# Int8 cross-attention stage of a two-layer Perceiver kernel: norm and queries made inside the stage, its context loaded during the FFN, transfers issued inside norms and attention, FFN units and turns in another order

## The chip, the cores and the metric

The kernel runs on one core of a Trainium2 chip. The metric is the device time of one execution in microseconds (us). The engines are named as in the profile: PE (TensorE), DVE (VectorE), ACT (ScalarE), POOL (GpSimd) and SP (SyncE, which only issues transfers here).

## What is computed

Two layers work on 256 tokens of 512 features, with a context of 4096 rows of 512 features. Each layer is a cross-attention over the context, a self-attention and an FFN, each behind a layernorm and with a residual.

```
x = x + L0_xattn(ln(x), ctx)   # fp8 projections, 16 heads of 128; self part (8 groups) and context part
x = x + L0_attn(ln(x))         # causal, 16 heads of 128
x = x + L0_ffn(ln(x))          # MXFP8 blocks of 32, 512 -> 2048 -> 512
x = x + L1_xattn(ln(x), ctx)   # int8, 16 heads of 32
x = x + L1_attn(ln(x))         # lightning attention with decay
x = x + L1_ffn(ln(x))          # mixture of 32 experts
```

The int8 attention, in whose stage most of the change lies:

```
q = x @ Wq + bq ; k, v = split(cond @ Wkv + bkv) ; q = q * 32**-0.5
q, k = fq_sym(q, per row of 32), fq_sym(k, per row of 32) ; v = fq_sym(v, per column over the context)
attn = fq_unsigned(softmax(q k^T), per row, 255 levels)
out  = (attn @ v) @ Wp + bp
```

## The kernel before

The program is a chain of stages. A stage allocates its SBUF and PSUM tiles and its semaphores, runs one block with a queue of instructions for each engine, and ends with a clearing of its semaphores and a barrier of all engines (`Stage.__exit__`). A plain block ends in a barrier too. Within a block engines meet only at semaphores, and each executes its queue in the order written.

The stages that the change touches, in order of time:

- `self_attention_stage` (self part of the first cross-attention, 133 to 198 us). A stage `ctx_load` stands ahead of it, whose block only has SP issue five transfers: the first weights and the 8 MB context for the wide stage.
- `wide_cross_attention_stage` (199 to 1172 us). 8 groups of 2 heads by 8 chunks of 512 context rows give 64 steps n; a step on PE is half of the key and value projection of chunk n, the transposes of chunk n-1's keys, the other half, `weigh` of chunk n-10, and the scores of chunk n-1. In the last group (n from 56) only keys are projected and the values come ten steps later. DVE measures and normalises keys, subtracts peaks (`shift`), keeps a running maximum (`top`), adds sums from step 66, and rounds 24 units of the later FFN's weights, each in two halves (`scale_unit`, `round_unit`) in successive steps. The halves stand in steps whose number modulo 8 is 4 to 7, 0 or 1, from step 4 to step 65. Units 21 to 23 are in steps 60 to 65. ACT copies projections and scores out of PSUM and takes roots and exponentials. POOL adds exponentials. SP loads a unit, stores it when it is rounded, and reloads q and the weights for each group.
- `build_middle`: a block that only issues the causal stage's first seven transfers; `layernorm_stage` "ln1"; the causal attention; "ln2"; `ffn_stage`. The FFN has 8 steps: `gate_up(n)` on PE, an exponential on ACT, 13 DVE instructions which end in a rounded tile, `turn` (4 transposes) and its copy, and `down(n)`. Turns 0 and 1 are of the FFN's input, and `gate_up(0)` waits for both.
- `build_int8_attention`: stage `ctx2`, whose block issues ten transfers (query, key and value weights and again the 8 MB context) while DVE clears `qrows`; `layernorm_stage` "ln3"; `int8_queries_stage` (query product, rounding, three copies as parts, 32 transposes, copies to `qrows`); `int8_cross_attention_stage`, then the projection.

In `int8_cross_attention_stage` all engines walk one list, `int8_order`. It opens with the first chunk's keys and values: for n from 0 to 7 a key product of 512 rows (PE) into the one PSUM tile `vp`, its bias add ("key kept") and rounding (DVE), its parts (ACT and POOL), a value product (PE), its copy (ACT) and peak (DVE), and from n = 3 the transposes of the keys of three steps before. The next key product waits for the last "key kept". Then come scores ("first": a maximum on DVE; "second": an exponential on ACT).

Of the kernel before, what the change touches and what calls it, by code (L numbers as in the profile page):

```python
# [162 lines left out]
def self_attention_stage(nc, C, qT, kT, v, inv_smooth, cat):  # L163
# [5 lines left out]
    with Stage(nc, "self") as st:  # L169
# [15 lines left out]
        with nc.Block() as block:  # L185

# [91 lines left out]
def wide_cross_attention_stage(nc, C, ctxT, s_ctx, w, s_w, wkv_dram, q_dram, vecs, inv_smooth, cat, units, early):  # L278
# [19 lines left out]
    UPG = FFN_EARLY // NG  # L298
    with Stage(nc, "wide") as st:
# [32 lines left out]
        with nc.Block() as block:  # L332

            @block.sync
            def _(sp):
# [9 lines left out]
                for g in range(NG):  # L345
                    if g >= 1:
                        sp.wait_ge(s_s, 4 * QPG * g)
                    sp.dma_start(q[:, :], q_dram[:, 2 * g:2 * g + 2, :].rearrange("p h n -> p (h n)")).then_inc(s_ql, 16)
                    if g + 1 < NG:
                        if g >= 1:  # L350
                            sp.wait_ge(s_a, 2 * QPG * g)
                        sp.dma_start(w[(g + 1) % 2][:, :, :], wkv_dram[g + 1]).then_inc(s_w[(g + 1) % 2], 16)
                    for i in range(UPG * g - 1, UPG * g + 2):
                        if i >= 0:
                            store_unit(i)
                        else:
                            load_unit(0)
                        if i + 2 < FFN_EARLY:
                            load_unit(i + 2)
                store_unit(FFN_EARLY - 1)  # L360
# [194 lines left out]
            def _(dve):  # L555
# [81 lines left out]
                for n in range(N + LAG + 1):  # L637
# [401 lines left out]
def ffn_stage(nc, C, xn, weights, x):  # L1039
# [3 lines left out]
    with Stage(nc, "ffn") as st:  # L1043
# [15 lines left out]
        with nc.Block() as block:  # L1059
# [42 lines left out]
            def _(pe):  # L1102
# [8 lines left out]
                def gate_up(n):  # L1111
                    f, t = steps[n]
                    pe.wait_ge(s_c, 2)
# [30 lines left out]
def build_middle(nc, C, A, x, early):  # L1144
    with ExitStack() as memory:
        weights = memory.enter_context(nc.sbuf_tensor("ffn_weights", [P, FFN_UNITS, 4, P], F32))
        with ExitStack() as inner:
            def sb(name, shape):
                return inner.enter_context(nc.sbuf_tensor(name, shape, F32))
            wqkv = [sb(f"causal_wqkv{e}", [P, 3, KC, 2 * D]) for e in range(2)]  # L1150
# [1829 lines left out]
```

## Time and profile before

| what | value |
|---|---|
| median of 3 runs | 2665.2 us (2664.5 to 2669.4) |
| profiled execution, its own time | 2665.4 us |
| its span, first to last instruction | 2663.6 us |
| mean granted TensorE clock | 0.943 |
| PE busy | 2332.8 us (88%) |
| DVE busy | 1805.9 us (68%) |
| ACT, POOL busy | 1247.5 us, 503.4 us |

The profiled execution takes 1.8 us beyond its span. Shares are means over stages with different limits, so the stages are read one by one. A clock of 1.00 is 2.4 GHz and of 0.50 is 1.2 GHz.

### The profile page before, as it was taken

To read this page: it belongs to the slowest core of one execution; us is meant where nothing else is said; L and a number is where in the kernel's file an instruction comes from. 1 tells how busy PE (TensorE), PEld (TensorE's weight loads), DVE (VectorE), ACT (ScalarE), POOL (GpSimd) and SP (SyncE) were. 2 spreads that over 40 slices of the span, in tenths; PEclk is the share of its full clock that TensorE was granted. 3 is DMA by queue.
4 is the path that set the end of the run, shared out by engine and by line. 5 is a ranking of instruction groups with operands and counts; after the bars stand their busy time and mean duration, and the time that the engine had idled before them with its cause. 6 is when DMAs were issued, how large, how long until landed. Compare 5 with 4: busy or idle time off the path is not lost. (4 is left out here: it accounts for less than half of the span.)

```text
span 2663.6 us, 32567 instructions
## 1 busy us (share of the span) xinstructions
PE 2332.8 (88%) x11672; PEld 1591.9 (60%) x11672; DVE 1805.9 (68%) x3552; ACT 1247.5 (47%) x2201; POOL 503.4 (19%) x411
## 2 busy tenths in 40 slices
PE   3679999999999999877996969887888879899998
PEld 2556766666666665545773346555545437677776
DVE  7754766777777689986785946767777753464444
ACT  4443466666566666432442104666666863211111
POOL 7710033333333334320000002110102000000000
PEclk8879999999999999988997979999999969899999
DMA  3320100000000000024440030000000005466662
GB/s 136 111 125 20 36 8 28 25 12 28 16 28 9 28 20 9 16 93 164 170 143 0 0 155 10 1 10 1 6 5 1 1 20 194 157 227 231 226 227 77
DMA packets 47067, 184.89 MB, mean 69 GB/s; under 512 B 6272, under 2 KB 11136, under 8 KB 36672
## 3 DMA queue, kind: packets, MB, share of 16 engines
q1 hardware_dynamic: 46912, 182.86, 18.9%
q8 instruction: 93, 1.52, 0.2%
q14 instruction: 62, 0.51, 0.1%
HBM read 173.93 MB, written 8.91 MB: 69 GB/s over the span
## 5 line engine op out<-in xcount | busy, mean ns | idle before, releaser
L397 PE MATMUL wide_a<-wide_w,ctxT 128*128 128x256 f32 (+1 forms) x2048 | 437.3, 367 | 2.8 <-POOL wide_eps L366 2.8
L397 PEld LDWEIGHTS wide_a<-wide_w,ctxT 128*128 128x128 f32 x2048 | 368.4, 191 | 76.6 <-issue 36.0
L379 POOL TENSOR_TENSOR wide_sums<-wide_sums,wide_s 128x512 f32<-128x512 f32 x224 | 301.8, 1347 | 463.2 <-ACT wide_s L527 450.1
L422 PE MATMUL wide_scores<-wide_q,wide_keysT 128*128 128x512 f32 x512 | 238.9, 605 | 13.9 <-ACT wide_s L523 13.9
L1572 ACT ACTIVATE int_prob<-int_a,int_shift,qscale 128x512 uint8<-128x512 f32 x256 | 199.0, 786 | 104.3 <-PE int_a L1464 103.7
L432 PE MATMUL wide_o<-wide_s,wide_values 128*128 128x512 f32 x512 | 232.2, 597 | 3.5 <-ACT wide_s L527 3.5
L523 ACT COPY wide_s<-wide_scores 128x512 f32<-128x512 f32 x256 | 148.3, 585 | 173.6 <-PE wide_scores L422 163.7
L1653 DVE TENSOR_REDUCE int_peaks<-int_a 128x1 f32<-128x512 f32 x256 | 169.3, 684 | 55.3 <-PE int_a L1464 53.2
L1464 PE MATMUL int_a<-int_keys,qrows 96*128 96x512 bf16 x512 | 164.4, 404 | 38.7 <-DVE int_peaks L1653 31.3
L422 PEld LDWEIGHTS wide_scores<-wide_q,wide_keysT 128*128 128x128 f32 x512 | 87.9, 189 | 150.0 <-ACT wide_s L523 89.2
L585 DVE TENSOR_TENSOR wide_top<-wide_top,wide_s 128x512 f32<-128x512 f32 x240 | 165.5, 689 | 8.7 <-ACT wide_s L523 2.9
L561 DVE BATCH_NORM_STATS2 wide_stats<-wide_keys 128x6 f32<-128x128 f32 x256 | 61.6, 282 | 157.3 <-ACT wide_values L505 156.8
L2159 PEld LDWEIGHTS moe_bank<-moe_xb,moe_gate_up 128*128 128x128 f32 (+1 forms) x1536 | 162.0, 183 | 8.3 <-issue 8.3
L2159 PE MATMUL moe_bank<-moe_xb,moe_gate_up 128*128 128x96 f32 (+1 forms) x1536 | 162.6, 266 | 4.3 <-issue 4.3
L432 PEld LDWEIGHTS wide_o<-wide_s,wide_values 128*128 128x128 f32 x512 | 96.2, 191 | 99.4 <-issue 93.2
L598 DVE TENSOR_TENSOR wide_s<-wide_s,wide_peak_rows 128x2048 f32<-128x2048 f32 x64 | 148.3, 2318 | 0.7
L1418 PE MATMUL int_vp<-int_wk,ctxT_again 128*128 128x128 f32 x1024 | 133.1, 288 | 2.7 <-PEq L77 1.9
L1418 PEld LDWEIGHTS int_vp<-int_wk,ctxT_again 128*128 128x128 f32 x1024 | 129.4, 203 | 7.4 <-issue 3.8
L503 ACT COPY wide_keys<-wide_a 128x256 f32<-128x256 f32 x128 | 46.6, 364 | 173.0 <-PE wide_a L397 172.9
L527 ACT ACTIVATE wide_s<-wide_s 128x2048 f32<-128x2048 f32 x64 | 122.4, 1912 | 10.0 <-DVE wide_s L598 9.4
L1464 PEld LDWEIGHTS int_a<-int_keys,qrows 96*128 96x128 bf16 x512 | 44.0, 100 | 110.5 <-DVE int_peaks L1653 56.9
L1380 POOL TENSOR_TENSOR int_rest<-int_kf,int_parts 128x512 f32<-128x512 f32 x32 | 37.0, 1156 | 364.9 <-ACT int_parts L1544 364.7
(398 smaller groups left out, 4280.0 us busy)
## 6 DMA issues: line engine op xcount, KB each, us to landing
moe_gate_up<-hbm_m_gu SPq DMA_DIRECT2D x34, 1408.0 KB, 6.1
moe_down<-hbm_m_down_a SPq DMA_DIRECT2D x34, 512.0 KB, 6.9
causal_wqkv<-hbm_wqkv SPq DMA_DIRECT2D x8, 1536.0 KB, 6.6
ctxT<-hbm_ctxT SPq DMA_DIRECT2D x4, 2048.0 KB, 14.9
oproj_raw<-hbm_wproj SPq DMA_DIRECT2D x8, 1024.0 KB, 5.0
ctxT_again<-hbm_ctxT SPq DMA_DIRECT2D x4, 2048.0 KB, 17.8
moe_down<-hbm_m_down_b SPq DMA_DIRECT2D x34, 192.0 KB, 7.1
wide_unit<-hbm_ffn_units SPq DMA_DIRECT2D x24, 256.0 KB, 2.6
```

The lines of the kernel that those rows point to most:

```text
L379: ins = pool.tensor_tensor(sums[0][:, :], before, part[:, j, :], ALU.add)
L397: mm = pe.matmul(a[h][:, j, cols], ctxT[:, kc, t * P:(t + 1) * P], w[g % 2][:, kc, cols], start=(kc == 0), stop=(kc == KC - 1))
L422: pe.matmul(sp_[j % 2][:, :], keysT[:, j, :], q[:, :], start=True, stop=True).then_inc(s_s, 1)
L432: mm = pe.matmul(o[g % 2][:, :], values[m % VR][:, j, :], s[m % SR][:, j, :], start=(c == 0 and j == 0), stop=(c == QPG - 1 and j == 3))
L523: act.copy(s[n % SR][:, j, :], sp_[j % 2][:, :]).then_inc(s_se, 1)
L585: link(dve.tensor_tensor(top[:, :], before, s[n % SR][:, j, :], ALU.max))
L598: dve.tensor_tensor(s[m % SR][:, :, :], s[m % SR][:, :, :], peak_rows[:, :].unsqueeze(1).to_broadcast([P, 4, COLS]), ALU.subtract).then_in ...
L1418: mm = pe.matmul(vp[:, t * P:(t + 1) * P], ctxT[:, kc, i * P:(i + 1) * P], wk[:, kc, :], start=(kc == 0), stop=(kc == KC - 1))
L1464: pe.matmul(a[n % 4][:, :], qrows[0:3 * HD, h, t * P:(t + 1) * P], keys[0:3 * HD, h % HC, j * 512:(j + 1) * 512], start=True, stop=True).t ...
L1572: act.activation(prob[u % 4][:, j * 512:(j + 1) * 512], a[n % 4][:, :], ACT.Exp, bias=shift[:, u % NU:u % NU + 1], scale=qscale[:, t, h:h ...
L1653: dve.tensor_reduce(peaks[u % 2][:, j:j + 1], a[n % 4][:, :], AX.X, ALU.max).then_inc(s_ad, 1)
L2159: mm = pe.matmul(dst[0:m, j, :], wgu[i][:, kc, z * EI + f0:z * EI + f0 + m], xb[q % 2][:, kc, e % BATCH, :], start=(kc == 0), stop=(kc == ...
```

## The change

- The blocks that only issue transfers are gone: the context for the wide stage is issued inside the self-attention's block, the causal stage's first transfers inside "ln1", the int8 stage's context and first key and value weights inside "ln2", ahead of the FFN. The context has its own place in SBUF for it.
- `ctx2` with the clearing of `qrows`, "ln3" and `int8_queries_stage` are gone as stages. Their work stands in `int8_order` beside the first key and value tiles. The query weights (1 MB) and bias are now issued as the int8 stage begins. Two of the three copies of the rounded queries and half of the copies of turned tiles move to ACT.
- Wide stage: the unit halves fill steps 0 to 17 without a gap, then the same steps modulo 8 as before. They end in step 57. SP's loads and stores of units follow them.
- FFN: `gate_up(0)` waits for the first turn only, and `turn(1)` follows it. At the end `down(6)` is ahead of the last turn.

```diff
-    UPG = FFN_EARLY // NG
+    slots = [n for n in range(N) if n <= 2 * QPG + 1 or n % QPG not in (2, 3)][:2 * FFN_EARLY]
...
-                    turn, half = divmod(n - 4, 2)
-                    i = UPG * (turn // 4) + turn % 4
-                    if n >= 4 and turn % 4 < UPG and i < FFN_EARLY:
+                    if n in slots:
+                        i, half = divmod(slots.index(n), 2)
                         (scale_unit, round_unit)[half](i)
...
-                    pe.wait_ge(s_c, 2)
+                    pe.wait_ge(s_c, min(n, 1) + 1)
...
                 turn(0)
-                turn(1)
                 for n in range(len(steps)):
                     gate_up(n)
-                    if n >= 1:
-                        turn(n + 1)
+                    turn(n + 1)
                     if n >= 2:
                         down(n - 2)
+                down(len(steps) - 2)
                 turn(len(steps) + 1)
-                down(len(steps) - 2)
                 down(len(steps) - 1)
...
+            def context_loads(sp):
+                for kc in range(KC):
+                    sp.dma_start(ctxT[:, kc, :], A["ctxT"][:, kc, :]).then_inc(s_ctx, 16)
+                sp.dma_start(wk[:, :, :], A["x_wkv"][0, :, :, :P]).then_inc(s_wk, 16)
+                sp.dma_start(kbias[:, :], A["x_bk"][0]).then_inc(s_wk, 16)
+                sp.dma_start(wv[:, :, :], A["x_wkv"][0, :, :, P:]).then_inc(s_wv, 16)
+                sp.dma_start(vbias[:, :], A["x_bv"][0]).then_inc(s_wv, 16)
...
+            layernorm_stage(nc, "ln2", C, x, xT, xn=xn, loads=context_loads)
...
-    order = []
+    order = [("norm", 0, 0)]
     for n in range(ns):
         order += [("key product", 0, 4 * n + t) for t in range(4)]
-        order += [("key kept", 0, n), ("key rounded", 0, n)]
+        if n == 0:
+            order += [("x turned", 0, t) for t in range(NT)]
+        order += [("key kept", 0, n)]
+        if n == 0:
+            order += [("query product", 0, t) for t in range(NT)]
+        order += [("key rounded", 0, n)]
+        if n in (0, 1):
+            order += [("query rounded", 0, n)]
...
+        if n in (2, 3):
+            order += [("query turned", 0, 2 * (n - 2) + i) for i in range(2)]
...
+                def query_parts(t):
+                    act.wait_ge(s_qr, t + 1)
+                    act.copy(n3[t][:, :, 1, :], n3[t][:, :, 0, :])
+                    act.copy(n3[t][:, :, 2, :], n3[t][:, :, 0, :]).then_inc(s_qp, 1)
...
+                def round_queries(t):
+                    if t == 0:
+                        dve.wait_ge(s_wq, 32)
+                    dve.wait_ge(s_qm, t + 1)
+                    dve.tensor_tensor(y[t], xq[t][:, :], bq, ALU.add).then_inc(s_qk, 1)
+                    dve.wait_ge(s_qk, t + 1)
+                    link(dve.tensor_scalar(y[t], y[t], float(np.float32(HD**-0.5)), None, ALU.mult))
+                    whole = int8_round(dve, link, y[t], qstat[t], y[t])
+                    link(whole(y[t]))
+                    dve.tensor_copy(n3[t][:, :, 0, :], y[t].rearrange("p (h d) -> p h d", d=HD)).then_inc(s_qr, 1)
+                    link(dve.tensor_copy(qscale[:, t, :], qstat[t][:, 1, :]))
```

## Rows read from the trace of the kernel before

**Rows 1.** Busy time by stretch; columns: stretch, us, engines, clock, DMA share, GB/s.
```profile
450.00:500.00 50.00, 50.00 (x177) 31.41 (x176) 37.75 (x82) 30.33 (x45) 18.77 (x15) 1.00 0.04 11
...
1060.00:1080.00 20.00, 16.18 (x74) 10.90 (x73) 18.83 (x30) 12.05 (x17) 7.80 (x6) 0.91 0.08 27
...
1544.00:1580.00 36.00, 14.34 (x57) 8.77 (x58) 18.63 (x38) 2.35 (x4) 0.33 (x3) 0.72 0.72 286
1590.00:1600.00 10.00, 10.00 (x48) 6.42 (x47) 7.06 (x14) 1.19 (x2) 2.19 (x2) 1.00 0.01 2
1700.00:1800.00 100.00, 86.71 (x596) 56.43 (x595) 71.24 (x124) 66.11 (x129) 14.77 (x13) 0.93 0.03 7
```

**Rows 2.** Timeline at the self-attention's start; start, us, instructions, idle before.
```profile
130.30 0.33 SPq L2955 DMA_DIRECT2D wide_w<-hbm_wkvx  x1
...
133.97 0.61 POOL L195 COPY self_q<-qT 128x512 f32 x1 [17.56 <-POOLq L193]
```

**Rows 3.** Timeline around the block ahead of ln1.
```profile
1221.03 1.54 DVE L713 SCALAR_TENSOR_TENSOR x_res<-oproj_acc,wscale,x_res 128x512 f32<-128x512 f32 x2 [8.61 <-PE oproj_acc L725]
1223.49 0.33 SPq L1160 DMA_DIRECT2D causal_wqkv<-hbm_wqkv  x1
...
1227.38 0.69 DVE L135 BATCH_NORM_STATS2 ln_stats<-x_res 128x6 f32<-128x512 f32 x1 [4.81 <-PEq L1156]
...
1230.85 0.55 DVE L140 TENSOR_SCALAR ln_xn<-x_res,ln_mv,ln_rstd 128x512 f32<-128x512 f32 x1
...
1234.23 6.46 PE L860 MATMUL causal_proj<-xT,causal_wqkv 128*128 128x256 f32 x16 [1.47 <-PEq L77]
```

**Rows 4.** Landing times of the causal stage's first two weight transfers, 1.5 MB each.
```profile
DMA to landing us min/median/max: 6.4/8.6/10.9
```

**Rows 5.** Timeline of PE, steps 61 to 64 of the wide stage.
```profile
1044.41 1.95 PE L397 MATMUL wide_a<-wide_w,ctxT 128*128 128x128 f32 x16
...
1056.12 1.98 PE L422 MATMUL wide_scores<-wide_q,wide_keysT 128*128 128x512 f32 x4 [2.23 <-ACT wide_s L523]
1057.94 1.95 PE L397 MATMUL wide_a<-wide_w,ctxT 128*128 128x128 f32 x16
...
1071.24 2.48 PE L422 MATMUL wide_scores<-wide_q,wide_keysT 128*128 128x512 f32 x4 [3.82 <-ACT wide_s L523]
...
1085.89 0.60 PE L441 MATMUL wide_turned<-ident,wide_keys 128*128 128x128 f32 x4
1089.95 2.93 PE L432 MATMUL wide_o<-wide_s,wide_values 128*128 128x512 f32 x3 [3.46 <-ACT wide_s L527]
```

**Rows 6.** Timeline of DVE in step 61: a unit's second half, then measure.
```profile
1062.08 1.50 DVE L2882 TENSOR_SCALAR wide_out<-wide_unit 128x512 uint32<-128x512 uint32 x1
...
1068.97 0.48 DVE L561 BATCH_NORM_STATS2 wide_stats<-wide_keys 128x6 f32<-128x128 f32 x2
```

**Rows 7.** Timeline of the FFN's first and last step.
```profile
1428.54 1.11 PE L1108 MATMUL ffn_tp<-ident,ffn_deq 128*128 128x128 f32 x4 [6.53 <-DVE ffn_deq L752]
...
1435.21 1.28 ACT L1096 ACT_TABLE_LOAD   x1
...
1435.25 6.66 PE L1118 MATMUL ffn_gate<-ffn_weights,ffn_xT 128*128 128x512 f32 x8 [0.68 <-ACT ffn_xT L1086]
...
1441.74 3.60 PE L1118 MATMUL ffn_up<-ffn_weights,ffn_xT 128*128 128x512 f32 x8
...
1445.37 0.60 ACT L1096 ACTIVATE ffn_e_neg<-ffn_gate 128x512 f32<-128x512 f32 x1 [8.88 <-PE ffn_up L1118]
...
1532.51 1.12 PE L1108 MATMUL ffn_tp<-ident,ffn_deq 128*128 128x128 f32 x4 [6.92 <-DVE ffn_deq L752]
...
1533.42 8.72 PE L1126 MATMUL ffn_acc<-ffn_weights,ffn_hT 128*128 128x512 f32 x16
```

**Rows 8.** Timeline from the FFN's end to the int8 stage's start.
```profile
1542.17 1.28 DVE L1080 TENSOR_TENSOR x_res<-x_res,ffn_acc 128x512 f32<-128x512 f32 x2 [9.72 <-PE ffn_acc L1126]
...
1562.91 0.69 DVE L1231 TENSOR_TENSOR xq_y<-xq_mm,x_bq 128x512 f32<-128x512 f32 x1 [6.05 <-PE xq_mm L1215]
...
1566.96 1.35 DVE L1236 CAST xq_n<-xq_y 128x512 bf16<-128x512 f32 x3
...
1574.39 3.58 PE L1221 MATMUL xq_tp<-ident,xq_n 128*96 128x128 bf16 x32 [8.15 <-DVEq L1238]
...
1577.30 1.46 DVE L1241 COPY qrows<-xq_tp 96x1024 bf16<-96x1024 bf16 x2 [0.16 <-PE xq_tp L1221]
...
1579.85 5.44 PE L1418 MATMUL int_vp<-int_wk,ctxT_again 128*128 128x128 f32 x32 [1.89 <-PEq L77]
```

More of the change, by code:

```diff
@@ L1262, in count, with int8_cross_attention_stage @@
         return self.readers.count(who)
-def int8_cross_attention_stage(nc, C, A, ctxT, s_ctx, weights, qrows, qscale, outT):
+def int8_cross_attention_stage(nc, C, A, residual, ctxT, s_ctx, weights, outT):
     HD, HC, CC = 32, 4, 4
@@ L1299, in int8_cross_attention_stage @@
         sums = st.ps("sums", [P, TOK])
+        xt = [a[t][:, :].rearrange("p (k n) -> p k n", n=P) for t in range(NT)]
+        xq = a[2:4]
         o, r = vp[:, 0:TOK], vp[:, TOK:]
@@ L1316, in int8_cross_attention_stage @@
                 use_a[step] = len(use_a)
-            if what in ("turn", "key turned", "value turned"):
+            if what in ("turn", "key turned", "value turned", "query turned"):
                 use_b[step] = len(use_b)
@@ L1329, in int8_cross_attention_stage @@
                 done_a[use_a[step]] = ("act", counts["a act"])
-            if what in ("turn", "key turned", "value turned"):
-                who = "dve" if what == "turn" and cast_on_vector(x, i) else "act"
+            if what in ("turn", "key turned", "value turned", "query turned"):
+                who = "dve" if what == "turn" and cast_on_vector(x, i) or what == "query turned" and i % 2 else "act"
                 counts["b " + who] += 1
@@ L1461, in score @@
                     a_free(n)
+                    if what == "first" and u == 0 and j == 0:
+                        for i in range(2, 4):
+                            who, seen = done_b[use_b["query turned", 0, i]]
+                            pe.wait_ge(s_ba if who == "act" else s_bd, seen)
                     if what == "first" and u % 4 == 0:
@@ L1511, in _ @@
                     what, x, i = step
-                    if what == "key product":
+                    if what == "x turned":
+                        turn_x(i)
+                    elif what == "query product":
+                        query_product(i)
+                    elif what == "query turned":
+                        turn_queries(i)
+                    elif what == "key product":
                         key_product(x, i)
@@ L1582, in _ @@
                     what, x, i = step
-                    if what == "value kept":
+                    if what == "norm":
+                        roots()
+                    elif what == "x turned" and i == 0:
+                        keep_x()
+                    elif what == "query rounded":
+                        query_parts(i)
+                    elif what == "query turned" and i % 2 == 0:
+                        keep_queries(i)
+                    elif what == "value kept":
                         keep_values(x, i)
@@ L1685, in _ @@
                     what, x, i = step
-                    if what == "key kept":
+                    if what == "norm":
+                        norm()
+                    elif what == "x turned" and i == 1:
+                        keep_x()
+                    elif what == "query rounded":
+                        round_queries(i)
+                    elif what == "query turned" and i % 2:
+                        keep_queries(i)
+                    elif what == "key kept":
                         keep_key(x, i)
```

259 lines of the change are left out of this document (135 added, 124 removed).

## Prediction

> **What bounds the kernel now.** I read busy time by stretch first, because the share of PE over the whole span hides where PE waits. In the middle of the wide stage PE is busy for all of 50.0 us and DVE for 37.8 [rows 1]: PE is the bound, and DVE work can be added or removed there for nothing. Near the stage's end it turns round: from 1060 to 1080 PE is busy for 16.2 of 20 us and DVE for 18.8, and the granted clock falls to 0.91 [rows 1]. From 1544 to 1580 PE works 14.3 of 36 us and the clock is 0.72. This is the stretch of block, norm and queries ahead of the int8 stage. In that stage's opening PE is full again (10.0 of 10 us, DVE 7.1) [rows 1]. Then I read the timelines at each seam for what the next stage waits for. So the change must be counted in three ways: seams that vanish, DVE work that leaves a DVE-bound stretch, and PE work that enters a PE-bound one.
>
> **Block ahead of the self-attention.** SP issues from 130.30, and POOL, which opens the attention, starts at 133.97 [rows 2]. With the issue inside the block both start at once: 3.7 us, less a few tenths for POOL's loop entry, which the gap may contain. I take 3.3, with ends 2.5 and 3.7. The context is needed only in the next stage, over 60 us later, so its five issues and its 8 MB cost nothing.
>
> **Block ahead of ln1.** The residual is done at 1221.03 + 1.54 = 1222.57 and SP issues 0.92 later, but the norm's first instruction is at 1227.38 [rows 3]. It can start when SP does now: 3.9 us. What is late next: the first weights land 6.4 us after their issue at 1223.49, that is 1229.9 [rows 3, 4]; PE would want them at 1234.23 - 3.9 = 1230.3. The margin is 0.4 us. If they landed at the median of 8.6 the gain would be 2.1. I take 3.9, lower end 2.1.
>
> **Wide stage, units.** Three units leave steps 60 to 65 and go to steps 0 to 3, 10 and 11. A second half takes 1068.97 - 1062.08 = 6.9 us of DVE in step 61 [rows 6]. Behind it stands the measuring of the next keys, behind that ACT's root, behind that ACT's copy of scores, and PE waits for that copy. These waits are 2.23 us (step 61, behind a first half) and 3.82 us (step 62) [rows 5]. Step 61 without its wait is 1057.94 - 1044.41 - 2.23 = 11.3 us. The three steps from 1044.41 to 1085.89 take 41.5 us [rows 5]; at 11.3 each they would take 33.9. The difference, 7.6 us, is the two waits and about 1.6 us of low clock. The 3.46 us wait at 1089.95 is for an exponential that ACT runs only after the scores of that step [rows 5]: it has no unit in it and stays, but its low clock and a later DVE delay may give 0.9. I take 8.5 in all. The lower end is 2 (the waits move to another DVE item), the upper 12 (the 3.46 goes too). From step 65 on PE doesn't wait, so what is gained lasts to the stage's end. In the early steps the added halves meet a DVE that has a quarter of its time free [rows 1], and in steps 0 to 9 there is no exponential to subtract or add; SP has a whole step for each load. I cost them at nothing. Without that cover they would cost up to 3 x 6.9 x 2 = 41 us, if every half were as slow as this one.
>
> **FFN start.** `turn(0)` ends at 1428.54 + 1.11, its copy on ACT 0.6 like the exponential over the same 512 columns, so `gate_up(0)` can start at 1430.3 instead of 1435.25 [rows 7]. It takes 1435.25 to 1445.3, 10.0 us, of which the first eight matmuls, 6.66 against 3.60 for the next eight, run mostly at the low clock. It ends at 1440.3. Now `turn(1)` (0.7 to 1.1), its copy (0.6) and the 1.28 us table load, which lay under the matmuls, come after it, before the exponential: 1442.8 to 1443.3 against 1445.37 [rows 7]. That is 2.1 to 2.6, and up to 4 if the clock rises sooner. I take 2.6. The rest of the FFN is a DVE chain (8 steps from 1446.0 to 1532.5, 10.8 each), which just moves.
>
> **FFN end.** `turn(9)` waits for DVE until 1532.51 after 6.92 us of idle PE; then 16 matmuls take 8.72 [rows 7]. Eight of them (`down(6)`) now run inside the idle time, 3.4 us of it. After the turn there is its 0.6 us copy, then eight matmuls: at full clock 3.6, at low clock about 6.9. Ended at 1542.1 before, the end comes at 1537.8 to 1541.1. I take the middle with the clock low for as long as before: gain 3.0, ends 0.8 and 4.4.
>
> **Norm and queries in the int8 stage.** PE's first key product comes 1.1 us after the query stage's last copy (1577.30 + 1.46, 1579.85) [rows 8]. The FFN's residual ends at 1542.17 + 1.28 = 1543.45, so it can now come at 1544.55: 35.3 us go. The context is long there, having been issued about 125 us earlier. Into the opening, where PE is full, comes this work on PE: the transposes of x and a wait for their copies, 1.2 us; 16 query matmuls at full clock, 2 x 3.45 = 6.9 [rows 7]; 32 small transposes, 3.58 at mostly low clock [rows 8], so 1.8 at full. That is 9.9 us. The norm is hidden under the first key product: 1230.85 + 0.55 - 1227.38 = 4.0 us [rows 3] against 5.44 [rows 8]. Query weights, 1 MB issued at the stage's start, have some 7 us; 1.5 MB took 6.4 [rows 4]. On DVE each rounding is 1566.96 - 1562.91 + 0.45 + 0.2 = 4.7 us with one copy for three [rows 8]. With three 0.7 us copies DVE gets 11.5 us into the first 35, of which it has nearly a third free. But they come in lumps. Behind the second rounding on DVE stand a value peak and the third tile's "key kept"; on ACT, behind the parts that wait for it, stand the first value copy and the second part of keys that POOL and DVE wait for. Key product 3 waits for them. Walking the list with these durations, PE reaches key product 3 at 28.4 us and DVE frees it at 29.6; the turned queries then hold the two PSUM tiles for another 0.8. I take 2.0 for stalls, with ends 0 and the two whole roundings, 9.4. So 35.3 - 9.9 - 2.0 = 23.4, ends 16 and 25.4. The memset of `qrows` is gone with the block and counts in the 35.3.
>
> **Sum.** 3.3 + 3.9 + 8.5 + 2.6 + 3.0 + 23.4 = 44.7 us. From the profiled execution's own 2665.4 (span 2663.6 and 1.8 around it), which stands 0.2 above the median, that gives 2620.7.
>
> **Rivals.**
>
> (a) The clock stays at its upper level where stages now follow one another. PE idles 3.5 us instead of 6.9 at the FFN's end, and 2.4 us ahead of the int8 stage, whose first key product of 32 matmuls took 5.44 [rows 8] where 16 of the same shape take 1.95 at full clock [rows 5]. Gains: 1.4 more at the FFN's end, 1.5 at the key product, 1.4 at the FFN's start: 2616.4. For it: the loss of these idle stretches. Against: from 1544 to 1580 the clock was 0.72 [rows 1], and a start from rest remains in the norms.
> The Trainium skill, TensorE: Matmul & The Clock Gate, "What's actually happening", says that the reduced clock is the default and that activity releases it. By that rule this rival gains and the forecast, which keeps every low stretch as it was, is too slow by these 4.3 us; the 0.72 in a stretch with PE idle for 60% agrees with it.
>
> (b) The queries stall the opening: both roundings and the parts behind them fall on PE's path, 9.4 instead of 2.0 us. 2628.1. For it: one PSUM tile for key products, and ACT's queue is in order. Against: PE has value products to do between.
>
> (c) The wide stage's end keeps its waits, gain 2 instead of 8.5: 2627.2. For it: DVE has other work to put in the units' place, the pieces of the finished group among it. Against: the chain from the unit to PE's wait is in the rows.
>
> (d) Slower: the attention that follows the int8 opening, some 520 us with PE 87% busy and a granted clock of 0.93 [rows 1], falls into a pattern with more low clock because its engines enter it in another phase. It has to eat 45 us. With PE on the path all the time, 45 of 520 is a clock of 0.85 in place of 0.93: from there on the kernel isn't faster, and at 0.83 it is 2676. Against: the list of steps there is unchanged.
>
> (e) The change does nothing because the early context load delays the stages it now lies beside, and the seams' gain is given back: 2665. Against: the same 8 MB came at 286 GB/s [rows 1] beside norm and queries, and their DVE instructions took the same 0.69 us as elsewhere [rows 8].
>
> **From cases to numbers.** Forecast 0.56, (a) 0.14, (b) 0.12, (c) 0.12, (d) 0.04, (e) 0.02. The likeliest case gives 2620.7, its own range 2614 to 2627. The range has to hold (a) to (c), two of them together, and the terms' ends: all lower ends give 2.5 + 2.1 + 2 + 2.1 + 0.8 + 16 = 25.5, all upper ends 53.4. Not all fall on one side, so I take 2608 to 2635. 0.2% is 5.3 us, about what a measurement of this kernel can tell from no change. Slower is (d), 0.04. Within 0.2% are (e) and a weak form of (d), which takes back about what the rest gains, 0.03 together. Faster: 0.93.
>
> **What the profile after would show.** POOL's first copy of the self-attention some 3.5 us sooner; the norm of ln1 0.9 us behind the residual; no step from 61 to 63 of the wide stage above 11.6 us; in the FFN, a table load directly before the first exponential and PE idle about 3.5 us before the last turn; the first key product about 1.1 us behind the FFN's residual; from there to the first scores about 12 us more than before. Wrong would be: a long wait of PE for "key kept" 2 or 3, the query weights landing after the turned x, the causal projection waiting for its weights, or a clock below 0.9 in the int8 attention.

## The result and the profile after

The changed kernel takes 2642.8 us (median of 4 runs, 2642.1 to 2644.0) beside 2667.1 for the kernel before on the same chip: a ratio of 0.991, 95% interval 0.9892 to 0.9927. It is faster, by 24 us where 44.7 were forecast, and lies outside the range of 2608 to 2635. The profiled execution took 2642.4 us with a span of 2640.6, so 23.0 us less span than before.

I laid the two traces side by side at the points where one stage hands over to the next. The gain up to each point, in us (time of the event before minus time after), and what it was since the last one:

| point | before | after | gain so far | this stretch | forecast |
|---|---|---|---|---|---|
| self-attention, POOL's first copy | 133.97 | 131.67 | 2.3 | 2.3 | 3.3 |
| ln1, first statistics | 1227.38 | 1214.48 | 12.9 | 10.6 | 8.5 + 3.9 |
| ln2, first statistics | 1416.63 | 1404.78 | 11.85 | -1.05 | 0 |
| FFN, first DVE instruction | 1423.47 | 1425.06 | -1.6 | **-13.4** | 0 |
| FFN's residual | 1542.17 | 1536.84 | 5.3 | 6.9 | 2.6 + 3.0 |
| int8 stage, first exponential | 1656.9 | 1628.8 | 28.1 | 22.8 | 23.4 |
| residual of its projection, first DVE instruction | 2190.4 | 2167.8 | 22.6 | -5.5 | 0 |
| last instruction | 2663.6 | 2640.6 | 23.0 | 0.4 | 0 |

Most terms came near what was forecast. One stretch that the forecast doesn't mention lost 13.4 us. It is the norm ahead of the FFN, in whose block SP now issues the context. The timeline of SP there, in the changed kernel (start, us, engine, line, operation, tiles, and in later rows in brackets the idle time before it and its releaser):

```profile
1404.69 2.01 SPq L1182 DMA_DIRECT2D ctxT_again<-hbm_ctxT  x4
1406.75 0.66 SPq L1183 DMA_DIRECT2D int_wk<-hbm_x_wkv  x1
1407.45 0.68 SPq L1184 DMA_DIRECT2D int_kbias<-hbm_x_bk  x1
1408.17 3.00 SPq L1185 DMA_DIRECT2D int_wv<-hbm_x_wkv  x1
1411.21 12.97 SPq L1186 DMA_DIRECT2D int_vbias<-hbm_x_bv  x1
```

And the timeline of DVE at the same place:

```profile
1410.48 0.69 DVE L143 COPY xT<-ln_tp 128x512 f32<-128x512 f32 x1 [1.41 <-PE ln_tp L159]
1425.06 0.69 DVE L746 TENSOR_REDUCE ffn_stat<-xn 128x16 f32<-128x512 f32 x1 [13.88 <-PEq L77]
```

DVE finishes the norm at 1411.2 and then waits 13.88 us at the end of the block (the line named is the stage's exit). The releaser that the profile names is PE's sequencer, but PE itself is idle too from 1411.2 to 1424.2. The row that ends just ahead of DVE's start is SP's: the issue of the value bias, 0.5 KB, takes 12.97 us and ends at 1424.18. In the stage where these transfers were issued before, the same value bias went out in 0.62 us. There the context came last:

```profile
1547.05 0.62 SPq L1766 DMA_DIRECT2D int_vbias<-hbm_x_bv  x1
1547.72 2.18 SPq L1768 DMA_DIRECT2D ctxT_again<-hbm_ctxT  x4
```

A reader who only looks at what waits finds a semaphore here. One who lists what every engine does inside the gap finds SP.

The wide stage's end on PE, to be read beside [rows 5]:

```profile
1042.23 1.95 PE L402 MATMUL wide_a<-wide_w,ctxT 128*128 128x128 f32 x16
...
1053.22 1.99 PE L427 MATMUL wide_scores<-wide_q,wide_keysT 128*128 128x512 f32 x4 [1.51 <-ACT wide_s L528]
...
1065.23 1.98 PE L427 MATMUL wide_scores<-wide_q,wide_keysT 128*128 128x512 f32 x4 [0.71 <-ACT wide_s L528]
...
1077.24 1.98 PE L427 MATMUL wide_scores<-wide_q,wide_keysT 128*128 128x512 f32 x4 [0.70 <-ACT wide_s L528]
1079.06 0.60 PE L446 MATMUL wide_turned<-ident,wide_keys 128*128 128x128 f32 x4
1083.12 5.40 PE L437 MATMUL wide_o<-wide_s,wide_values 128*128 128x512 f32 x8 [3.46 <-ACT wide_s L532]
```

The FFN's first step and its end, against [rows 7], and the int8 stage's opening, against [rows 8]:

```profile
1430.12 1.12 PE L1112 MATMUL ffn_tp<-ident,ffn_deq 128*128 128x128 f32 x4 [19.68 <-DVE ffn_deq L756]
1431.91 5.50 PE L1122 MATMUL ffn_gate<-ffn_weights,ffn_xT 128*128 128x512 f32 x8 [0.67 <-ACT ffn_xT L1090]
...
1530.37 0.66 PE L1112 MATMUL ffn_tp<-ident,ffn_deq 128*128 128x128 f32 x4 [3.54 <-DVE ffn_deq L756]
1531.70 5.10 PE L1130 MATMUL ffn_acc<-ffn_weights,ffn_hT 128*128 128x512 f32 x8 [0.68 <-ACT ffn_hT L1094]
1539.01 3.81 PE L1415 MATMUL int_vp<-int_wk,ctxT_again 128*128 128x128 f32 x32 [2.21 <-PEq L77]
...
1545.55 7.13 PE L1454 MATMUL int_a<-int_vq,int_prob 128*128 128x512 f32 x16 [1.86 <-DMA int_probT<-hbm_x_bq]
...
1568.42 3.84 PE L1415 MATMUL int_vp<-int_wk,ctxT_again 128*128 128x128 f32 x32 [0.83 <-DVE int_kf L1682]
...
1577.45 0.62 PE L1484 MATMUL int_b<-ident,int_parts 128*96 128x128 bf16 x8 [0.87 <-ACT int_qrows L1590]
1578.84 0.62 PE L1484 MATMUL int_b<-ident,int_parts 128*96 128x128 bf16 x8 [0.76 <-DVE int_qrows L1727]
```

The timeline of ACT in the FFN's first step shows the table load, which now lies bare between the second turn's copy and the exponential:

```profile
1441.32 0.59 ACT L1090 COPY ffn_xT<-ffn_tp 128x512 f32<-128x512 f32 x1 [9.46 <-PE ffn_tp L1112]
1441.92 1.28 ACT L1100 ACT_TABLE_LOAD   x1
1443.22 0.60 ACT L1100 ACTIVATE ffn_e_neg<-ffn_gate 128x512 f32<-128x512 f32 x1
```

### The profile page after: what moved, and what is told of

Its sections match the earlier page's. It is cut to its first block and busy times, and to the rows that moved or that the text cites. A ratio compares the mean times of both kernels' runs of the same rounds, so it can differ in the third digit from the quotient of the medians.

```text
span 2640.6 us, 32466 instructions
## 1 busy us (share of the span) xinstructions
PE 2326.4 (88%) x11672; PEld 1586.5 (60%) x11672; DVE 1799.9 (68%) x3545; ACT 1252.7 (47%) x2207; POOL 503.7 (19%) x411
## 5 line engine op out<-in xcount | busy, mean ns | idle before, releaser
L1633 ACT ACTIVATE int_prob<-int_a,int_shift,int_qscale 128x512 uint8<-128x512 f32 x256 | 199.1, 786 | 103.5 <-PE int_a L1499 102.9
L1499 PE MATMUL int_a<-int_keys,int_qrows 96*128 96x512 bf16 x512 | 166.0, 408 | 41.8 <-DVE int_peaks L1753 34.8
L1499 PEld LDWEIGHTS int_a<-int_keys,int_qrows 96*128 96x128 bf16 x512 | 44.4, 101 | 114.5 <-DVE int_peaks L1753 59.7
## 6 DMA issues: line engine op xcount, KB each, us to landing
ctxT<-hbm_ctxT SPq DMA_DIRECT2D x4, 2048.0 KB, 14.8
```

The costliest lines, as they stand in the source:

```text
L1499: pe.matmul(a[n % 4][:, :], qrows[0:3 * HD, h, t * P:(t + 1) * P], keys[0:3 * HD, h % HC, j * 512:(j + 1) * 512], start=True, stop=True).t ...
L1633: act.activation(prob[u % 4][:, j * 512:(j + 1) * 512], a[n % 4][:, :], ACT.Exp, bias=shift[:, u % NU:u % NU + 1], scale=qscale[:, t, h:h ...
```

## The experiments

The first theory for the 13.4 us: SP can't issue the small transfers while so much of the context is queued ahead of them, and the block of ln2 doesn't end before SP does. Its rival: the 8 MB delay by their traffic the norm and the FFN beside which they lie, in whatever order they are issued. The other runs ask what each part of the change is worth by itself, and what took 5.5 us from the int8 attention. Ratios are to the kernel before on the same chip. "Stretch" always means the time between two events of the profiled execution.

**Small transfers first.** The four small loads go ahead of the context; nothing else is changed.

```diff
             def context_loads(sp):
-                for kc in range(KC):
-                    sp.dma_start(ctxT[:, kc, :], A["ctxT"][:, kc, :]).then_inc(s_ctx, 16)
                 sp.dma_start(wk[:, :, :], A["x_wkv"][0, :, :, :P]).then_inc(s_wk, 16)
                 sp.dma_start(kbias[:, :], A["x_bk"][0]).then_inc(s_wk, 16)
                 sp.dma_start(wv[:, :, :], A["x_wkv"][0, :, :, P:]).then_inc(s_wv, 16)
                 sp.dma_start(vbias[:, :], A["x_bv"][0]).then_inc(s_wv, 16)
+                for kc in range(KC):
+                    sp.dma_start(ctxT[:, kc, :], A["ctxT"][:, kc, :]).then_inc(s_ctx, 16)
```

> The changed kernel with the four small loads (key and value weights and their biases) issued ahead of the context's four pieces in ln2's block. Theory (SP is held: the small loads queue behind 8 MB, the last issue takes 12.97 us, and ln2's end waits for SP): SP is done about 5 us after its first issue, the FFN's first DVE instruction comes about 12 to 13.5 us sooner, and the kernel takes 2629 to 2631. Rival (the 13.4 us between ln2's statistics and the FFN come from the context's traffic, whatever its order): no change, 2642. Rival (partly both): the FFN starts sooner, but its first instructions, now beside the transfer, are slower and give 3 us or more back: 2633 or more.

Measured: 2631.0 us, ratio 0.986 (0.9842 to 0.9877), span 2624.8. The timeline of SP in ln2:

```profile
1398.81 0.65 SPq L1181 DMA_DIRECT2D int_wk<-hbm_x_wkv  x1
...
1401.07 0.61 SPq L1184 DMA_DIRECT2D int_vbias<-hbm_x_bv  x1
1401.73 2.00 SPq L1186 DMA_DIRECT2D ctxT_again<-hbm_ctxT  x4
```

DVE, at the norm's end and the FFN's start:

```profile
1404.61 0.69 DVE L143 COPY xT<-ln_tp 128x512 f32<-128x512 f32 x1 [1.41 <-PE ln_tp L159]
1406.03 0.69 DVE L746 TENSOR_REDUCE ffn_stat<-xn 128x16 f32<-128x512 f32 x1 [0.73 <-PEq L77]
```

SP is done in 4.9 us, and DVE waits 0.73 in place of 13.88. From ln2's first statistics to the FFN's first instruction it is 7.1 us, against 20.3 in the changed kernel and 6.8 before. The whole 8 MB move beside the norm and the FFN as in the changed kernel, so their traffic costs this stretch at most 0.3 us: the rival falls. The FFN takes 1.3 us longer here than in the changed kernel, which lies in its last eight products at a lower granted clock (6.66 us against 5.10).

**The same order, issued where nobody waits.** To separate the order of the transfers from the barrier, the changed kernel's own order was kept and the function was called in the FFN's block.

```diff
-            layernorm_stage(nc, "ln2", C, x, xT, xn=xn, loads=context_loads)
-            ffn_stage(nc, C, xn, weights, x)
+            layernorm_stage(nc, "ln2", C, x, xT, xn=xn)
+            ffn_stage(nc, C, xn, weights, x, context_loads)
```

> The changed kernel with the context and the small loads, in the changed kernel's own order, issued in the FFN's block in place of ln2's. Theory (what cost 13.4 us is that ln2's block can't end before SP has issued): SP is held for some 13 us as before, but nobody waits for it; ln2's statistics to the FFN's first DVE instruction take 7 us in place of 20.3, and the kernel is as fast as with the small loads first (ratio 0.986). Rival (traffic beside the norm or the FFN costs time of itself): the FFN's first steps get slower by some us. Rival (the order alone matters): no gain.

Measured: 2631.1 us, ratio 0.9864 (0.9843 to 0.9885). The last rows of SP's timeline:

```profile
1413.68 2.89 SPq L1189 DMA_DIRECT2D int_wv<-hbm_x_wkv  x1
1416.61 14.26 SPq L1190 DMA_DIRECT2D int_vbias<-hbm_x_bv  x1
```

SP is held even longer, 14.26 us, and the kernel is as fast as with the small transfers first. The stretch from ln2's statistics to the FFN is 7.4 us, and from the FFN's first DVE instruction to its residual 113.6, as in the run before this one (113.7). So the hold by itself is free; it costs because a short block has to end on it.

**Half of the context first.** Two of its four pieces, then the small loads, then the other two.

> The changed kernel with two pieces of the context (4 MB), then the four small loads, then the other two pieces. If SP is held by the bytes that are queued ahead of an issue, the small loads are held about half as long or not at all, and the last two pieces somewhat: ln2's statistics to the FFN between 7 and 14 us. If it is small rows behind any large transfer that hold SP, about 20 us as in the changed kernel.

Measured: 2632.3 us (one run), span 2630.4. SP's timeline in ln2:

```profile
1401.33 0.80 SPq L1182 DMA_DIRECT2D ctxT_again<-hbm_ctxT  x2
...
1404.45 0.67 SPq L1186 DMA_DIRECT2D int_vbias<-hbm_x_bv  x1
1405.17 6.57 SPq L1188 DMA_DIRECT2D ctxT_again<-hbm_ctxT  x2
```

Now no small transfer is held. The two last pieces take 6.57 us together, but not alike; the view of the tile gives the shortest, median and longest issue in ns, and the first and last start:

```profile
L1188 SPq DMA_DIRECT2D ctxT_again<-hbm_ctxT x2: 441/3262/6082, 1405.2 to 1411.3; - x2
```

The third piece is held, 6.08 us, and the fourth follows in 0.44. The stretch from ln2's statistics to the FFN is 11.2 us, between 7.1 and 20.3.

**One small transfer behind the context.** Key and value weights and the key bias first, the value bias last.

> The changed kernel with three of the small loads ahead of the context and the last one, the value bias of 0.5 KB, behind its four pieces. Theory that any issue behind 8 MB is held: the last issue takes about 13 us, ln2's statistics to the FFN 20 us, the kernel 2643. Rival (SP is held only from the point at which enough is queued; behind the four pieces the first two small issues took 0.66 and 0.68 us in the changed kernel): the last issue takes under 1 us, the stretch 7 us, the kernel 2629 to 2632.

Measured: 2628.5 us (one run), span 2626.7. The last issue behind all four pieces:

```profile
1405.49 2.33 SPq L1185 DMA_DIRECT2D ctxT_again<-hbm_ctxT  x4
1407.87 0.47 SPq L1186 DMA_DIRECT2D int_vbias<-hbm_x_bv  x1
```

0.47 us, and the stretch is 7.1, as the rival expected. The same 0.5 KB behind the same 8 MB took 12.97 us in the changed kernel. So the first half of the theory was too simple: a large transfer ahead doesn't hold an issue by itself.

What differs is where the weights stand. Packets moved until the value bias is issued, first here (from 1403.00 to 1407.87), then in the changed kernel (from 1404.60 to 1411.21):

```profile
DMA packets 1202, 0.85 MB, mean 175 GB/s; under 512 B 47, under 2 KB 1184, under 8 KB 1184
DMA packets 131, 2.11 MB, mean 319 GB/s; under 512 B 1, under 2 KB 1, under 8 KB 1
```

Here 1184 small packets, those of the weights and the key bias, are moved by then, though the value weights land only 0.8 us later. There the weights still wait behind the context. Every long hold is of an issue that comes after weights which themselves wait behind pieces of the context. It ends when nearly all of the context ahead of them is moved: 7.7 of 8.4 MB in the changed kernel, 8.2 of 8.4 when issued in the FFN, 3.6 of 4.2 with half of it first.

Two simple counts are ruled out by the traces. The first is the bytes still to come. By an estimate, the sizes issued less what the profile shows as moved, they were 8.2 MB here at the issue of 0.47 us, and 3.8 MB with half of the context first, where the third piece was held. The second is the number of transfers not yet landed. It was six at that hold, and eight in the kernel before at the last piece of the context, whose issue took at most 0.75 us. Whether the number of rows or packets counts, and where, stays open.

**The FFN's order back.** `turn`, `gate_up` and `down` in the order of the kernel before, and `gate_up` waits for both turned halves again.

```diff
-                    pe.wait_ge(s_c, min(n, 1) + 1)
+                    pe.wait_ge(s_c, 2)
...
                 turn(0)
+                turn(1)
                 for n in range(len(steps)):
                     gate_up(n)
-                    turn(n + 1)
+                    if n >= 1:
+                        turn(n + 1)
                     if n >= 2:
                         down(n - 2)
-                down(len(steps) - 2)
                 turn(len(steps) + 1)
+                down(len(steps) - 2)
                 down(len(steps) - 1)
```

> The changed kernel with the FFN's order of turns, products and down projections of the kernel before. By the traces the new order gained 3.7 us at the start and 3.3 at the end, so this takes about 7 us more than the changed kernel. If the FFN's part was a shift of the table load and of waits alone, under 2 us.

Measured: 2648.9 us, ratio 0.9926 (0.9911 to 0.9941). The FFN, from its first DVE instruction to its residual's second, takes 117.2 us, against 112.4 in both profiles of the changed kernel, 113.7 in the one with the small transfers first, and 119.3 before. Against the changed kernel the order is worth 4.8 us: 2.3 at the start (21.1 against 18.8 us to the first exponential's reader on DVE) and 2.5 at the end (8.9 against 6.5 from the last turn to the residual). In all profiles with the new order the FFN takes 112.4 to 114.3 us, so the worth is 2.9 to 4.8: with the last eight products at the lower clock the end takes 8.0 us, and the order gains 0.9 there. The 2.1 us by which the same order took longer in the profile before lie in the granted clock: its first eight products took 6.66 us [rows 7] and here 5.23; its last sixteen 8.72 against 7.99.

**The units' steps back.** The wide stage's units in the steps of before; SP's order stays the new one.

```diff
-    slots = [n for n in range(N) if n <= 2 * QPG + 1 or n % QPG not in (2, 3)][:2 * FFN_EARLY]
+    slots = [n for n in range(4, N + LAG) if (n - 4) // 2 % 4 < FFN_EARLY // NG][:2 * FFN_EARLY]
...
-                for n in range(N):
-                    if n % QPG == 0:
+                for n in range(N + LAG):
+                    if n < N and n % QPG == 0:
```

> The changed kernel with the units of the wide stage in the steps in which they were before (SP's order is the new one). By the traces the wide stage gained 5.6 us, where the forecast had 8.5: so 5 to 6 us more than the changed kernel. If the gain came from SP's order and not from the steps of the units, none. If a part of the gain is taken back by something else that moved, 8 or more.

Measured: 2654.6 us, ratio 0.9947 (0.9933 to 0.9962). From its first to its last instruction the wide stage takes 972.8 us here, 972.6 in the first profile before and 975.9 in the second, against 967.2 in the changed kernel (967.1 to 969.2 in all eleven profiles with the new steps). The waits of PE from 1030 to 1110, by line and what was waited for (us in total, times, longest), in this kernel:

```profile
PE wide_scores L427 <- ACT wide_s L528: 7.2, 4, 3.8
PE wide_o L437 <- ACT wide_s L532: 3.5, 1, 3.5
PE wide_rows L454 <- DVEq L591: 2.3, 1, 2.3
```

The same waits in the changed kernel, from 1027 to 1105:

```profile
PE wide_scores L427 <- ACT wide_s L528: 4.6, 6, 1.5
PE wide_o L437 <- ACT wide_s L532: 3.5, 1, 3.5
PE wide_rows L454 <- DVEq L591: 1.5, 1, 1.5
```

These waits are 3.4 us shorter with the new steps of the units, and the stage 3.6 to 5.6. The old steps vary by themselves: in the second profile before, PE waits 11.3 us for the copies of scores, in place of 7.1. SP's order alone gave nothing that stands out of this spread.

**Both blocks back.** The transfers ahead of the self-attention and of ln1 are issued in blocks of their own again.

```diff
+                with nc.Block() as block:
+
+                    @block.sync
+                    def _(sp):
+                        loads(sp)
+
-                self_attention_stage(nc, C, qT, kT, v, inv_smooth, cat, loads)
+                self_attention_stage(nc, C, qT, kT, v, inv_smooth, cat, None)
...
+                with nc.Block() as block:
+
+                    @block.sync
+                    def _(sp):
+                        loads(sp)
+
-                layernorm_stage(nc, "ln1", C, x, xT, loads=loads)
+                layernorm_stage(nc, "ln1", C, x, xT)
```

> The changed kernel with both transfer blocks back, ahead of the self-attention and ahead of ln1. By the traces they were worth 2.3 and 3.9, but the causal stage gave 1.0 back, which may be the price of weights issued beside the norm: 5 to 6.5 us more than the changed kernel. By the forecast's terms 7.2.

Measured: 2648.6 us, ratio 0.9921 (0.9906 to 0.9936), beside 0.9908 (0.9889 to 0.9927) for the changed kernel in another set of runs, so the times alone leave it open. The profile doesn't. At the self-attention:

```profile
130.76 0.33 SPq L3040 DMA_DIRECT2D wide_w<-hbm_wkvx  x1
...
134.18 0.61 POOL L201 COPY self_q<-qT 128x512 f32 x1 [17.22 <-POOLq L199]
```

POOL starts 3.4 us behind SP, where in the changed kernel it starts 0.5 behind it (131.67 and 131.18). At ln1 DVE stands idle for 4.80 us ahead of the first statistics, as before (4.81), against 0.97. Together 2.9 and 3.8, some 6.8 us. The causal stage is 187.3 us here and 186.4 to 188.7 in the kernels without the blocks, so the 1 us it seemed to cost in the changed kernel is within its spread.

**Both kernels again.** Unchanged, for a second profile of each.

> The kernel before, once more, for a second profile. The int8 stage from its first to its last exponential took 513.7 us in the first profile of before and 519.1 to 522.4 in the five profiles of the changed kernel and its variants. Theory (the granted clock's pattern is the price of the new opening, or of what stands ahead of it): again 513 to 515. Rival (the pattern differs from execution to execution, and the first profile was a short one): 518 to 522, and then the changed kernel gave nothing back here.

> The changed kernel once more, on the chip of these runs, so that the variants are compared beside it. By its first timing a ratio of 0.991 to before. Its stretch of exponentials in the int8 stage: 519 to 522 by the theory that it belongs to the kernel; anything from 513 to 522 by the rival that it is chance.

Measured: 2672.0 us (one run) for the kernel before; 2644.6 us for the changed one, ratio 0.9908 (0.9889 to 0.9927). The exponentials took 517.4 us in the kernel before, 3.7 more than in its first profile and less than in any of the changed kernel; in the changed one 521.3. For the kernel before that is between the two expectations; for the changed one it fits both. The two groups stand apart by less than they first did.

**The int8 stage back.** Small transfers first, and norm, queries and int8 attention as before the change.

```diff
-        int8_cross_attention_stage(nc, C, A, x, *context, outT)
...
+        with queries:
+            layernorm_stage(nc, "ln3", C, x, xT)
+            int8_queries_stage(nc, C, wq, bq, s_wq, xT, qrows, qscale)
+        int8_cross_attention_stage(nc, C, A, ctxT, s_ctx, (wk, wv, kbias, vbias, s_wk, s_wv), qrows, qscale, outT)
...
-    order = [("norm", 0, 0)]
+    order = []
```

> The changed kernel with the small loads first, but with norm, queries and int8 attention as in the kernel before (the context is loaded in ln2's block still). Theory: from the FFN's residual to the first exponential 113 to 114 us in place of 90 to 91, and the stretch of exponentials at 513.7 to 517.4 like both profiles of before, in place of 519.1 to 522.4: some 17 us slower than with the new int8 stage, 2647. Rival (the longer attention is chance or comes from the stages ahead): a stretch of 519 or more here too, 2652.

Measured: 2643.1 us, ratio 0.9911 (0.9894 to 0.9929). From the FFN's residual to the first exponential 110.4 us (90.2 with the new stage, 114.2 before the change): so by the profiles the new stage is worth 20.2 and what the early load of the context takes out of the old one 3.8. The times give less, as the profiled execution was the slowest of six (2649.3 us): the median is 14.8 us above that of the kernel with the queries' bias early (next run), timed beside it, where 17 were expected. The exponentials took 518.6 us. That is the old list of steps, and it is 4.9 us longer than in the first profile before. Whole stretches of the exponentials, by the view of stretches (us, engines, granted clock, DMA share, GB/s), first in the kernel before:

```profile
1657.00:2170.00 513.00, 421.10 (x2987) 255.45 (x2985) 381.85 (x677) 365.60 (x712) 54.56 (x48) 0.93 0.01 3
```

In the changed kernel:

```profile
1629.00:2148.00 519.00, 422.70 (x2986) 255.89 (x2984) 382.11 (x677) 366.71 (x714) 54.61 (x48) 0.93 0.01 3
```

And with the int8 stage back:

```profile
1636.00:2154.00 518.00, 424.25 (x2985) 258.03 (x2984) 381.99 (x677) 365.82 (x712) 54.54 (x48) 0.93 0.01 3
```

DVE and ACT do the same work to within 1.2 us, and the granted clock is 0.93 in all three. PE's busy time differs by up to 3.2, and the rest is waiting.

**The queries' bias early.** Small transfers first, and the bias of the queries among them.

```diff
+            bq = sbr("int8_bq", [P, DM])
+            s_wq = nc.alloc_semaphore("query_weights_loaded")
...
+                sp.dma_start(bq[:, :], A["x_bq"]).then_inc(s_wq, 16)
```

> The changed kernel with the small loads first and the queries' bias among them, so that at the int8 stage's start only the 1 MB of query weights is to come. The first query product waited 1.86 us for the bias in the changed kernel, but only 0.33 us, for a copy on ACT, with the small loads first: so 2629 to 2631, no more than 0.3 us gained over those. If the bias still costs something behind the weights, 1 to 2 us.

Measured: 2628.3 us, ratio 0.9861 (0.9839 to 0.9882): nothing gained over the small transfers first, as expected. Its first key product:

```profile
1522.23 3.81 PE L1415 MATMUL int_vp<-int_wk,ctxT_again 128*128 128x128 f32 x32 [2.21 <-PEq L77]
```

**PE starts late.** Small transfers first, and one more wait ahead of the first key product.

```diff
                 pe.wait_ge(s_ctx, 16 * KC)
+                pe.wait_ge(s_wq, 32)
```

> The small loads first, and PE waits for the query weights before its first key product, which starts it 4 to 5 us later and with the norm already done. It changes nothing in the list of steps of the attention. Theory (the attention's low-clock stretches hang on the phase in which PE enters it): the opening gets 2 to 5 us longer and the first 48 exponentials take another time than 53.1, somewhere from 49.6 to 54.5. Rival (the new stage itself makes the attention slower, whatever its phase): 53 to 54.5 again, and the whole stretch 519 to 522.

Measured: 2633.6 us (one run), span 2631.8. The first key product comes 6.7 us behind the residual in place of 1.5, and the first exponential 95.7 in place of 90.2. From the first exponential to the 25th it takes 53.1 us, exactly as without the delay (the expectation counts these 24 as 48, with the instruction that reads each one's sum), and all of them 520.8. Entering 5 us later changed nothing: with one profile of each, this speaks against the theory that the phase in which PE starts the stage decides.

## Why the prediction was wrong, and where it was right

**The step that failed** is the one that isn't in its sum: the price of moving the context's issue into ln2's block. The forecast listed the context as "issued about 125 us earlier", asked of the new place only whether its traffic would slow the neighbours (rival (e), 2 in 100), and counted none of the eight issues as an instruction of SP in a block that the FFN waits for. The four small transfers are issued behind the context in the new function, where they went ahead of it before. That is a change of order in the diff which the forecast didn't read as one. It measured 13.4 us: 20.3 in place of 6.8 from the norm's statistics to the FFN. With the order turned back, the kernel ran at 0.986, some 2628 us on the 2665.2 of before, which is inside the range. The range had no room for such a step: all lower ends of the terms give 25.5 us, 2640, and 2642.8 lies beyond even that.

**The wide stage** was right in mechanism and by the two first profiles 3 us too large in size: 5.4 against 8.5. (The spread of either kernel's stage allows 3.4 to 8.8.) The step at fault is "at 11.3 each". It took step 61 without its wait as the length of a step without a unit. But the steps that now carry none still wait 1.51, 0.71 and 0.70 us for the copy of scores on ACT. So the part from 1044.41 to 1085.89 [rows 5], 41.5 us, became 1079.06 - 1042.23 = 36.8 and not 33.9. The two named waits, 6.05 us, were not gone but shortened.

**The seams.** At ln1 3.9 us were forecast and 3.8 came. The weights landed in time: the first projection starts 6.85 us behind ln1's first statistics, before (1234.23 - 1227.38) and after. At the self-attention 3.3 were forecast; against a kernel with the block back POOL starts 2.9 us sooner relative to SP. The 2.3 of the table contains the differences of all that lies ahead.

**The FFN.** Start: 2.3 us by the run with the order back (2.6 forecast, the upper end of its own 2.1 to 2.6); end: 2.5, or 0.9 with the clock low (3.0 forecast, ends 0.8 and 4.4). In the two first profiles it looked like 3.7 and 3.2, the start because in the changed kernel the clock rose sooner (first eight products 5.50 against 6.66 us). The table load stands bare ahead of the exponential, and PE idles 3.54 us ahead of the last turn, as said.

**The clock, rival (a).** The rival names three places and 4.3 us, and in both profiles of the changed kernel it came in all three: the FFN's first eight products took 5.5 us against 6.66, its last eight 5.1 where the low clock has 6.66, and the first key product 3.81 against 5.44 [rows 8], some 4.4 us. The table holds them in its FFN and int8 stretches. The kernel with the small transfers first, with the same instructions there, had the low level at the last two places, and the one with the bias early had 3.81 again:

```profile
1512.42 6.66 PE L1130 MATMUL ffn_acc<-ffn_weights,ffn_hT 128*128 128x512 f32 x8 [0.68 <-ACT ffn_hT L1094]
1521.29 5.44 PE L1415 MATMUL int_vp<-int_wk,ctxT_again 128*128 128x128 f32 x32 [2.21 <-PEq L77]
```

The two places go together. Of the nine profiles with the new FFN order and the new int8 stage entered without a delay, six have 5.1 to 5.4 us for the last eight products and 3.81 for the key product, three have 6.6 to 6.8 and 5.44.
The Trainium skill, TensorE: Matmul & The Clock Gate, "What's actually happening", has the reduced clock as the default which activity releases. The traces agree in kind, but the same matmuls behind the same 2.21 us of idle gave both levels, so it is no term to add to a sum.

**The int8 opening** was forecast to gain 23.4 and gained 22.8. That it came so near is in part luck, as the parts were less exact. Sixteen query products took 7.13 us against 6.9; the forecast's 3.45 for eight isn't in [rows 7], which show 3.60. PE met four waits, 1.86 (the queries' bias), 0.83 (key product 3, forecast at 1.2 + 0.8 with the tiles), 0.87 and 0.76 (the PSUM tiles of the turned queries): 4.3 us against 2.0. The first key product at the upper clock gave 1.6 of that back. The long wait of rival (b) didn't come.

**The int8 attention** was forecast unchanged and took 5.4 us more in the two first profiles. All profiles with the old list of steps: 513.7, 517.4, 518.6. All eleven with the new stage ahead of it: 519.1 to 522.4. What is shown: 3.7 us appear between two executions of the same kernel, and up to 4.9 with no change in this stage's code. What isn't settled is whether the remaining small difference is the stage's, and what picks the pattern: the delayed start left it as it was. Rival (d) was right that this stage could get longer, at an eighth of the 45 us that it needed; that it does so by more low clock isn't shown, as the granted clock is 0.93 in every row above.

The sum, in us, by the table's stretches: forecast 44.7; less 1.0 (self), 1.8 (wide stage to ln1: 10.6 for 12.4), 1.0 (causal), 13.4 (SP held), 0.6 (opening) and 5.5 (int8 attention) is 21.4; more 1.3 from the FFN and 0.4 at the end is 23.1, and 23.0 is measured. The wide stage's missing 3.1 appear as 1.8 because the stage behind it, which no edit touches, took 48.5 us in place of 49.9 (48.3 to 50.2 in the others).

**The best version** here is the change with the small transfers first, 0.986 of the kernel before. With the queries' bias among them it is the same, 0.9861, and so it is with the transfers issued in the FFN's block, 0.9864.

## What to carry to other kernels

When transfers move into another block, count their issues as instructions of SP in that block, in their order, and ask who waits for the block's end; a short norm is a bad place for whatever can be held. Put the small transfers ahead of the large, or issue all of them in a long block in which SP has nothing else to do. And where a wait is removed, the gain goes only down to the next wait behind it: take the step's length from a step that has neither, or keep the removed waits as the upper bound.

## What the runs showed of the hardware

An issue on SP isn't of fixed price. The same 0.5 KB transfer took 0.47, 0.61 and 0.62 us to issue in three orders, and 12.97 or 14.26 where weights of short rows stood behind the eight megabytes and ahead of it. With half of the context first, a piece of the context was held instead, 6.08 us. The bytes of the context and of its small transfers are the same in all these orders.
The Trainium skill, DMA: Bandwidth & Descriptors, "Issuing engines are not separate DMA queues", calls the time to initiate a DMA usually small relative to the DMA itself. Here that held for the value bias where nothing held SP: 0.62 us to issue, and 2.6 us or more from issue to landing later in the changed kernel. In the held rows the issue alone took 12.97 us.

The stage of self-attention, with the same instructions in it, took 61.2 us in one kernel and 66.6 in another, at a granted clock of 0.86 and 0.79. First the stretch with the small transfers first:

```profile
130.88:192.12 61.24, 45.99 (x192) 34.87 (x192) 36.35 (x96) 29.08 (x84) 11.50 (x25) 0.86 0.35 146
```

And in the second profile of the kernel before:

```profile
132.26:198.86 66.60, 50.48 (x192) 38.41 (x192) 36.36 (x96) 29.24 (x84) 11.51 (x24) 0.79 0.29 123
```

Such steps of 2 to 5 us in stretches that no edit touches are as large as most terms of this change. They are why its parts were read from the stretches that they touch, and not from the kernels' times.
